# DLRM tower on one core: second dots of the last whole unit in one piece, first unit's first layer later, compares against chunk numbers in PSUM

## What is computed

```python
e = jnp.stack([tbl_0[ids[:, 0]], ..., tbl_25[ids[:, 25]]], axis=1)
T = jnp.concatenate([r_dense[:, None, :], e], axis=1)      # 2048 x 27 x 128
Z = jnp.einsum('bnd,bmd->bnm', T, T)
z = Z[:, iu0, iu1]                                          # the 351 pairs
h = jnp.concatenate([z, r_dense], axis=1)
h = jnp.maximum(h @ W_top1 + b_top1, 0.0)                   # 479 -> 512
h = jnp.maximum(h @ W_top2 + b_top2, 0.0)                   # 512 -> 256
y = h @ W_top3                                              # 256 -> 1
```

## Time and profile before

| what | us |
| --- | --- |
| median of 3 runs | 370.04 (368.55 to 371.23) |
| the profiled execution | 370.17 |
| its span on the core | 368.4 |
| TensorE matmuls busy | 344.3 |
| VectorE busy | 222.6 |
| ScalarE busy | 171.6 |
| GpSimd busy | 255.0 |

### The profile page before, as it was taken

One profiled execution on the slowest core, in us unless ns is written; L12 is line 12 of the kernel. 1 busy time (PEld: TensorE's weight loads), 2 busy tenths in 40 slices (PEclk: granted clock), 3 DMA queues, 4 the chain that ended last, 5 costly groups with the idle time before them and its releaser, 6 DMA issues.

```text
span 368.4 us, 9930 instructions
## 1 busy us (share of the span) xinstructions
PE 344.3 (93%) x4044; PEld 319.9 (87%) x4044; DVE 222.6 (60%) x815; ACT 171.6 (47%) x220; POOL 255.0 (69%) x263
## 2 busy tenths in 40 slices
PE   3998798879999999999999999999999999996997
PEld 1887698769899899999999899999999899995896
DVE  4989969876447485467457484557448484514131
ACT  5267736551463624661563534662463534362511
POOL 6778777787777777777777777777777777772000
PEclk9999999989999999999999999999999999999999
DMA  7997242354522551236322551236321532254130
GB/s 202 261 243 200 65 131 60 83 140 107 186 61 56 133 169 50 60 86 157 118 59 53 140 169 50 59 91 150 121 59 52 133 101 53 60 126 108 31 43 20
DMA packets 45878, 39.07 MB, mean 106 GB/s; under 512 B 32930, under 2 KB 39113, under 8 KB 45834
## 3 DMA queue, kind: packets, MB, share of 16 engines
q1 hardware_dynamic: 36014, 21.40, 22.1%
q0 software_dynamic: 8192, 16.79, 18.2%
q10 hardware_dynamic: 1628, 0.25, 0.5%
HBM read 32.40 MB, written 6.02 MB: 104 GB/s over the span
## 4 chain that ended last, share of the span: by engine, by line
PE 75%; DVE 8%; DMA 7%; SPq 5%; issue 2%; ACT 2%; DVEq 0%
PE look_ps L770 32%; PE mlp_ps L817 13%; PE gram_ps L797 12%; PE look_ps L780 6%; PE mlp_ps L827 6%; DVE hot L476 4%; DMA dots<-gram 3%; PE look_ps L761 3%; SPq L331 2%; SPq L346 2%; DMA w<-in_tbl_dram 2%; DVE tab_lo L458 1%; DMA w<-in_W_top_dram 1%; SPq L351 1%; DMA pairs<-dots 1%
## 5 line engine op out<-in xcount | busy, mean ns | idle before, releaser
L427 POOL DMA_INDIRECT rows<-in_tbl_dram,ids_all x240 | 237.6, 990 | 73.1 <-issue 72.2
L476 DVE TENSOR_SCALAR hot<-ids_near 125x256 fp32r<-125x256 f16 x640 | 150.1, 304 | 65.5 <-PE look_ps L770 60.3
L770 PE MATMUL look_ps<-hot,tab_hi 125*128 125x256 f32 x616 | 154.8, 291 | 7.1 <-DVE hot L476 3.6
L770 PE MATMUL look_ps<-hot,tab_lo 125*128 125x256 f32 x616 | 150.5, 284 | 0.0
L770 PEld LDWEIGHTS look_ps<-hot,tab_hi 125*128 125x128 f32 x616 | 118.5, 192 | 10.2 <-ACT T L628 3.6
L770 PEld LDWEIGHTS look_ps<-hot,tab_lo 125*128 125x128 f32 x616 | 118.7, 193 | 0.1
L628 ACT COPY T<-look_ps 128x384 f32<-128x384 f32 (+1 forms) x80 | 79.1, 1091 | 20.3 <-PE look_ps L780 19.3
L620 ACT COPY T<-look_ps 128x512 f32<-128x512 f32 x32 | 38.3, 1197 | 103.3 <-PE look_ps L770 62.7
L797 PEld LDWEIGHTS gram_ps<-T 128*54 128x54 f32 x2048 | 53.9, 130 | 9.2 <-DVE gram L500 2.6
L797 PE MATMUL gram_ps<-T 128*54 128x54 f32 x2048 | 57.7, 214 | 3.4 <-DVE gram L500 2.3
L500 DVE COPY gram<-gram_ps 128x486 f32<-128x486 f32 (+1 forms) x64 | 37.9, 598 | 17.0 <-DMA dots<-gram 8.5
(11 more groups left out here) (74 smaller groups left out, 145.5 us busy)
## 6 DMA issues: line engine op xcount, KB each, us to landing
dots<-gram SPq DMA_DIRECT2D x28, 182.2 KB
ids_near<-ids_rows SPq DMA_DIRECT2D x7, 640.0 KB, 5.9
rows<-in_tbl_dram,ids_all POOLq DMA_INDIRECT x240, 2.5
T<-in_tbl_dram SPq DMA_DIRECT2D x5, 448.0 KB
pairs<-dots SPq DMA_DIRECT2D x14, 117.0 KB
rows<-in_r_dense_dram SPq DMA_DIRECT2D x16, 64.0 KB
gram<-in_tbl_dram SPq DMA_DIRECT2D x2, 448.0 KB
pairs<-dots SPq DMA_DIRECT2D x7, 104.0 KB
```

The source lines that it names most:

```text
L427: pool.indirect_dma_start(rows[:, t % 2, place[n], :], None, tables[n - 1], bass.IndirectOffsetOnAxis(ap=index[:, n - 1:n].bitcast(U32), a ...
L476: eq = nc.vector.tensor_scalar(hot[:VP, at % 2, c], ids_near[:VP, u % 2, k], float(c), None, ALU.is_equal)
L770: mm = pe.matmul(dst, w[:VP, k, c], hot[:VP, slot, c], start=(c == 0 and half == 0), stop=(c == CH - 1 and half == 1))
```

## The change

1. In unit 6 the dots of tile 1 are made in one piece on TensorE, all four pieces ahead of look 3, and VectorE copies all four before compares 8 and 9.
2. In unit 1 the first steps of layer 1 of unit 0 come behind turn 2 and look 2; ScalarE's `h1_out` moves with them.
3. From unit 3 on, compares 0, 1, 2 and 4 to 8 (eight of the ten) are one instruction over 125x2048 that compares `ids_near`, repeated for the chunks, with the chunk numbers 0 to 7. These lie in eight columns of bank 1 of `gram_ps`, behind the columns that the dots use, and are written once by VectorE, after the compares of unit 0. Each is read 256 times in a row.
4. Since the dots' odd pieces write to that bank, TensorE waits before them until the compares that read it are done, and VectorE's order becomes: two copies, two compares, two copies, with compares 3 and 9 in the old form.

```diff
+        steps = gram_ps[:, 1, 500:500 + CH]
...
+        def by_steps(u, at):
+            return u >= 3 and at not in (3, 9)
...
-                for c in range(CH):
-                    eq = nc.vector.tensor_scalar(hot[:VP, at % 2, c], ids_near[:VP, u % 2, k], float(c), None,
-                                                 ALU.is_equal)
+                if by_steps(u, at):
+                    if u == 3 and at == 0:
+                        dve.wait_ge(steps_ready, CH)
+                    near = ids_near[:VP, u % 2, k:k + 1].to_broadcast([VP, CH, Q])
+                    eq = nc.vector.tensor_tensor(hot[:VP, at % 2], near, steps[:VP].rearrange(
+                        "p (c q) -> p c q", q=1).to_broadcast([VP, CH, Q]), ALU.is_equal)
+                else:
+                    for c in range(CH):
+                        eq = nc.vector.tensor_scalar(hot[:VP, at % 2, c], ids_near[:VP, u % 2, k], float(c), None,
+                                                     ALU.is_equal)
...
+            dve.wait_ge(ids_t_ready, UNITS)
+            for c in range(CH):
+                nc.vector.memset(steps[:, c:c + 1], float(c)).then_inc(steps_ready, 1)
             compare(1, 0)
...
-                for b in range(BLOCKS):
-                    gram_out(u, 0, [b])
-                    compare(u + 1, 2 + b)
+                gram_out(u, 0, (0, 1))
+                compare(u + 1, 2)
+                compare(u + 1, 3)
+                gram_out(u, 0, (2, 3))
+                compare(u + 1, 4)
+                compare(u + 1, 5)
...
+                if u + 1 < END:
+                    gram_out(u, 1, (0, 1))
+                    compare(u + 1, 8)
+                    compare(u + 1, 9)
+                    gram_out(u, 1, (2, 3))
+                    compare(u + 2, 0)
+                    compare(u + 2, 1)
+                else:
+                    gram_out(u, 1)
+                    compare(u + 1, 8)
+                    compare(u + 1, 9)
...
+                if t == 0 and b == 0:
+                    pe.wait_ge(steps_ready, CH)
+                if b % 2 == 1 and 1 < u < END:
+                    pe.wait_ge(hot_ready, K * (u + 1) + (2 if l == 0 else 8) + (b == 3 and (l == 0 or u + 1 < END)))
...
-                layer1(u - 1, 0, 8)
+                if u > 1:
+                    layer1(u - 1, 0, 8)
                 turn(u, 1, 2)
                 look(u + 1, 2)
-                layer1(u - 1, 8, 12)
+                layer1(u - 1, 8 if u > 1 else 0, 12)
...
+                if u + 1 < END:
+                    products(u, 1, 0)
+                    products(u, 1, 1)
+                    look(u + 1, 3)
+                    products(u, 1, 2)
+                    products(u, 1, 3)
+                else:
+                    for b in range(BLOCKS):
+                        products(u, 1, b)
+                    look(u + 1, 3)
```

More of the change, by code:

```diff
@@ L95, in dlrm_tower @@
     assert VP * CH == V and VP <= P and V <= 2048 and D == P and F1C == 4 and F2C == 2 and K % 2 == 0
-    assert NV % 2 == 1 and MC * PC == NV and KP <= P and 18 * NV <= 512 and dense_round == NR - 1
+    assert NV % 2 == 1 and MC * PC == NV and KP <= P and 18 * NV <= 500 and dense_round == NR - 1
     w1_pieces = pair_weight_pieces(NV, HALF, MC)
@@ L187, in dlrm_tower @@
         dense_ready = sem("dense_ready")
+        steps_ready = sem("steps_ready")
         gram_done = sem("gram_done")
@@ L719, in _ @@
                 turn_out(u, 1, 1)
-                h1_out(u - 1, 0)
+                if u > 1:
+                    h1_out(u - 1, 0)
                 turn_out(u, 1, 2)
                 look_out(u + 1, 2)
+                if u == 1:
+                    h1_out(u - 1, 0)
                 turn_out(u, 1, 3)
```

## The result

The changed kernel takes 365.22 us (364.58 to 365.76, 4 runs) where the kernel before takes 370.51 us in the same session (368.55 to 371.23, 4 runs): ratio 0.9865, 95% interval 0.9821 to 0.9909. It is faster by 1.35%. The forecast was 367.0 us with "within 1%" as the likeliest case, and a range that ended at 365.7 us.

A forecast was written before the change was run, and what follows sets the result against it. The prediction took TensorE's matmuls as the bound, with DMA waits for pairs and weights removable. Tail -2.55, weights' wait -0.9 and writes +0.3 gave -3.15 us: 370.17 to 367.0 us, own range 366.0 to 368.2, with rivals 365.7 to 369.4.

The forecast's parts named there:

- within 1%: Whole kernel: time within 1% (3.7 us) of the kernel before, chance 0.64; faster by over 1% 0.28, slower 0.08.
- TensorE is the bound, full units stay: Full units: matmuls fill 41.16 of 41.27 us; longer compares still end 0.3 to 0.5 us in time, cost 0.
- Compares of 2.30 us: VectorE's new compares: one instruction over 2048 elements takes 2.30 us, 0.43 us longer than before.
- rival (c): New compares: repeated PSUM reads run at two cycles an element, 4.4 us a compare, some 385 us in all; chance 0.08.
- The new wait before look 4: Unit 6's end: TensorE waits 0.7 us for compare 8, which the dots no longer hide.
- Tail, -2.55: Unit 6's end: one-piece dots remove the wait for pairs before layer 1, gain 2.55 us, bounds 1.9 and 3.25.
- First layer, -0.9: Unit 1: layer 1 of unit 0 placed later no longer waits for weights, gain 0.9 us, bounds 0.6 and 0.9.
- Eight writes, +0.3: After unit 0's compares: writing chunk numbers takes 0.7 us, making TensorE wait 0.3 us before piece 2; bounds 0 and 0.8.
- Rival (a): Whole kernel: no new waits, compare shorter or sooner and writes hidden, 366.0 us; chance 0.18.
- The 366.3 us for a compare at the old rate: New compares: with the old rate kept, some 1.3 us each, no wait before look 4, sum 366.3 us.
- Rival (b): Unit 6's end: the tail gives its gain back through shared queues or another late load, 369.6 us; chance 0.12.

The follow-up runs named there:

- V1: Kernel before with only the tail change (unit 6's second dots in one piece, old compares): 365.14 us against 369.01 us, single runs, undisturbed.
- W1: Kernel before with only the first layer of unit 0 moved behind turn 2 and look 2: 367.59 us, ratio 1.0013, undisturbed.
- W2: Kernel before with only the new compares, chunk numbers, waits and copy order: 366.76 us, ratio 0.9983, undisturbed.
- W4: The kernel before, unchanged, timed again as the others: 367.56 us, ratio 1.0012, undisturbed.
- T1: Kernel before with only the tail change (unit 6's second dots in one piece): 594.99 us, ratio 0.9965, in a disturbed session.
- T3: Kernel before with only the new compares, chunk numbers, waits and copy order: 582.83 us, ratio 0.9784, in a disturbed session.
- T4: The changed kernel again, against the kernel before: 582.03 us, ratio 0.9801, in a disturbed session.
- U3: Kernel before with only the new compares, chunk numbers, waits and copy order, in a second disturbed session: 580.82 us, ratio 0.9757.
- Z1: The changed kernel with a dummy write ahead of each new compare: 580.3 us, ratio 1.0 against the kernel before, in a disturbed session.

## Why the prediction was right or wrong, step by step

The result is 1.8 us under the forecast of 367.0. Between the two profiled executions, whose spans differ by 4.6 us, the sum of steps (-3.15) can be checked term by term. (The prediction's own range should have ended at 368.5 by its bounds, -1.9 - 0.6 + 0.8, not at 368.2; nothing hangs on it.)

- **TensorE is the bound, full units stay.** Right: 41.29 us, and 206.35 to 206.43 over five units in seven executions, although VectorE works 2.8 us more per unit (forecast 3.4). The margins are as argued. In the unit from 206 us the compare ahead of piece 3 ends at 210.01 + 2.29 = 212.30, and piece 3 is due about 212.7 (211.75 and half of the two pieces); VectorE's timeline:

```profile
210.01 2.29 DVE L488 TENSOR_TENSOR hot<-ids_near,gram_ps 125x2048 fp32r<-125x2048 f16 x1 [1.55 <-PE look_ps L803]
```

and TensorE's:

```profile
211.75 2.01 PE L835 MATMUL gram_ps<-T 128*54 128x54 f32 x72
```

- **Compares of 2.30 us.** Right, 2.285; rival (c), two cycles per element, is dead. The new wait before look 4 was 0.63 us (forecast 0.7); V1 shows which half of it each part brings.
- **Tail, -2.55.** Mechanism right, size short: -2.94 (33.49 to 30.55), inside its bounds of 1.9 to 3.25. The new wait was near (0.63 for 0.7); the removed one was mis-sized. I let the turn end at its start + 0.66, and the row says 2.95 us of wait. But matmuls overlap: without the wait layer 1 starts 0.49 us behind the turn's start, and its first block takes 1.46, not 1.56 us. So the removed wait was 339.28 - 335.67 - 0.49 = 3.12 us, plus 0.1. And the wait before piece 2 of unit 7's first dots fell from 0.46 to 0.18 us, where I had taken off 0.13; W1, W2 and W4 have 0.18 too, with the old tail, so this was chance of the one execution and not the change.
- **First layer, -0.9.** The step from look 0 of unit 2 to unit 1's second dots went from 23.42 to 22.27 us, -1.15, for the same reason (the row's 0.89 leaves out the overlap, 0.16, and the slower first block, 0.1). But its premise, that this wait belongs to the kernel, failed: W4 and V1, with layer 1 in its old place, don't have it, and W1 gains nothing in its median.
- **Eight writes, +0.3.** Wrong in price: eight writes took 0.12 us, not 0.7. I had priced them by the distance of two small casts. The 0.3 us of wait before piece 2 did not come. TensorE's first dots took 3.65 us after 3.50, so at most 0.15 on the path; the rows below, of W2 with the same writes and then of V1 without them, differ by 0.10:

```profile
43.88 3.65 PE L833 MATMUL gram_ps<-T 128*54 128x54 f32 x128 [0.47 <-ACT T L647]
```

```profile
44.06 3.55 PE L801 MATMUL gram_ps<-T 128*54 128x54 f32 x128 [0.52 <-ACT T L620]
```
- **What no step named.** The changed execution's first dots came 0.35 us sooner (44.40 to 44.75). The table says that this is chance (43.65 to 44.95 whatever the kernel). And its profiled execution lies 0.36 us above its own median.

Sum: 0.39 (tail) + 0.25 (weights) + 0.48 (0.3 forecast for the writes, where the stretch from first dots to look 0 of unit 2 became 0.18 shorter) + 0.35 + 0.36 = 1.83 us, the miss but for 0.03. The steps that failed are three sizes in the sum: the tail at -2.55, of which the removed wait was 3.12 + 0.1 and not 2.95 us; the weights' wait at -0.9, which measured -1.15; and the eight writes at +0.3, which cost 0.15 at most. Together these sizes make 0.65 us of the miss. The other 1.2 us are differences between executions: the wait before piece 2, the rest of the stretch behind the first dots (38.9 to 39.7 us in the seven profiles, with the writes or without), the earlier first dots and the 0.36.

A further step failed, and it concerns the gain more than the time: "Forecast 370.17 - 3.15 = 367.0 us" takes one execution's waits for DMAs as fixed. They are not: the wait for pairs was 1.88 to 2.98 us in the four profiles with the old tail, the one for weights 0.8 to 0.9 in two and none in two that have the old order of layer 1. The kernel before took 367.0 (35 runs) and 370.5 us, the changed kernel, which has neither wait, 365.2 in both sessions. The gain is thus 1.8 us in one session and 5.3 in the other; one profile of the kernel before could not have told which. Why the kernel before was slower in the first session was not shown. The lower clock behind the pairs' wait alone is not it: the profile of 370.17 us has 0.995, and in the fourth session no execution of a kernel with the old tail took more than 369.0 us at that clock.

Rival (a), no new waits, gave 366.0 us and was nearest to the time, for a wrong reason: the new wait is there. The 366.3 us for a compare at the old rate came near by luck as well: it took 2.285 us, not 1.3. Rival (b), the tail gives its gain back, fell: the pairs land some 4 us ahead of their use.

## What to carry to other kernels

A wait for a DMA in one profile is a draw, not a constant: take a second profile before pricing its removal, and price it by start to start (the next instruction's start behind the one before, as elsewhere in the timeline), which here gives 0.3 us more than the bracketed idle time. A longer instruction on an engine with slack cost nothing here, where each consumer's due time had been checked; I take the tightest margin (here 0.4 us) as the number to watch rather than the engine's idle share, but no run went past it undisturbed. Removing idle time of TensorE can also remove a lower clock behind it (11 of 71 executions with the wait, none of 12 without).

## What the runs showed of the hardware that was not expected

- In four of seven sessions the same programs take 573 to 597 us instead of 365 to 370. It is not the chip: on one and the same chip the fourth session was undisturbed and the fifth, minutes later, disturbed. TensorE's mean granted clock is 0.80 to 0.83 in the profiles, and it idles some 90 to 115 us for "issue" in front of single matmuls of the dots (107 times in T1); in the undisturbed traces "issue" is 0.2 to 0.4 us at a time. The new compares bring 13 to 15 us there (T3, T4, U3), where the same edit is worth nothing undisturbed (W2). They mean 543 VectorE instructions instead of 815, but the number alone does not explain it, since Z1 with 583 took as long as the kernel before. That all engines' instructions come late through something shared is my guess; no run tested it.
- A wait of 1.9 us was followed by the lower clock (W2), one of 2.16 us in unit 1 too (after), and waits of 2.4 and 2.95 us were not (W1, before). The length of the idle time alone does not decide.
- Eight writes of 128x1 back to back took 0.12 us, 59 ns each by the trace with overlap, where the two casts of the earlier trace rows stand 0.09 us apart.
- A write of 1024 16-bit zeros stands in the trace as 512 32-bit ones, in 0.485 us.
